# A macaron block on one core: three of four rounds of state powers on GpSimd, slots laid out anew, first constants on ScalarE's queue, the flag read ahead of the last store

## What is computed

```
K = s4d_kernel(log_dt, log_A_real, A_imag, C_real, C_imag, 1024)   # 256 channels x 32 states -> 1024 taps
def conv(x):   y = irfft(rfft(x, 2048) * rfft(K, 2048))[:1024]; return gelu(y) @ W.T + b
def ffn(x):    h = silu(x @ w1.T * s1) * (x @ w2.T * s2)           # 256 -> 1024
               h = gelu(h @ h1.T * t1); h = gelu(h @ h2.T * t2)    # 1024 -> 1024 -> 1024
               return h @ w3.T * s3                                # 1024 -> 256
x = x + 0.5 * ffn(layernorm(x))
x = x + conv(layernorm(x))
x = x + 0.5 * ffn(layernorm(x))
```

## Time and profile before

| | |
|---|---|
| median of 3 runs | 1340.68 us (1340.23 to 1342.07) |
| the profiled execution's own time | 1344.0 us |
| its span, first to last instruction | 1342.2 us |
| mean granted TensorE clock | 0.994 |
| busy: PE, DVE, ACT, POOL | 1318.8, 893.0, 746.7, 382.9 us |

### The profile page before, as it was taken

How to read it: one execution, slowest core, us unless ns; L and a number is a source line. 1 busy time by engine, 2 the same in 40 slices (tenths; PEclk the granted TensorE clock), 3 DMA queues, 4 the chain that set the end, 5 groups by cost and what they waited for, 6 DMA issues and landing times.

```text
span 1342.2 us, 18334 instructions
## 1 busy us (share of the span) xinstructions
PE 1318.8 (98%) x7278; PEld 670.6 (50%) x7278; DVE 893.0 (67%) x1746; ACT 746.7 (56%) x1201; POOL 382.9 (29%) x350
## 2 busy tenths in 40 slices
PE   8999999799999999999999999999999999999997
PEld 3454454455544445455454554545545455454544
DVE  5257869842543877878778787787877873454723
ACT  5474546564447456574665746757467464445422
POOL 5811129500010442614326043260532500001000
PEclk9999999899999999999999999999999999999999
DMA  9210001001010000000100000000000001222300
GB/s 335 97 47 9 9 1 17 1 1 17 0 48 17 0 17 1 9 9 0 17 0 9 16 9 17 17 9 16 9 16 17 9 17 71 69 89 53 136 0 18
DMA packets 44701, 41.88 MB, mean 31 GB/s; under 512 B 32704, under 2 KB 41408, under 8 KB 41920
## 3 DMA queue, kind: packets, MB, share of 16 engines
q1 hardware_dynamic: 44608, 40.64, 10.4%
HBM read 28.57 MB, written 4.19 MB: 24 GB/s over the span
## 4 chain that ended last, share of the span: by engine, by line
PE 92%; DVE 6%; ACT 1%; DMA 1%; issue 1%; SPq 0%; DVEq 0%
PE psf L1339 62%; PE psf L1327 16%; PE psf L1351 8%; PE pss L1402 2%; DVE arena L585 2%; PE pss L1412 2%; PE pss L1392 2%; DVE arena L588 1%; DVE hab L626 1%; PE pss L1382 1%; DMA g<-w 1%; PE pss L1367 0%; DVE arena L597 0%; DVE arena L804 0%; ACT sil L1094 0%
## 5 line engine op out<-in xcount | busy, mean ns | idle before, releaser
L1339 PE MATMUL psf<-hab,wall 128*128 128x512 f16 x4096 | 890.8, 379 | 5.0 <-DVE ht L638 3.1
L1339 PEld LDWEIGHTS psf<-hab,wall 128*128 128x128 f16 x4096 | 399.2, 98 | 486.5 <-issue 7.9
L1111 ACT ACTIVATE psf<-psf,scf 128x512 f32<-128x512 f32 x256 | 168.7, 659 | 428.9 <-PE psf L1339 428.8
L626 DVE SCALAR_TENSOR_TENSOR hab<-psf,hab 128x512 f16<-128x512 f32 x256 | 175.4, 687 | 307.8 <-ACT hab L1104 307.6
L1327 PE MATMUL psf<-h,wall 128*128 128x512 f16 x1024 | 236.1, 384 | 8.3 <-DVE hab L626 6.9
L1327 PEld LDWEIGHTS psf<-h,wall 128*128 128x128 f16 x1024 | 100.5, 99 | 127.0 <-DVE hab L626 8.2
L1104 ACT ACTIVATE hab<-psf 128x512 f16<-128x512 f32 x256 | 152.9, 597 | 8.1
L975 POOL TENSOR_SCALAR rs<-mv 128x4 f32<-128x4 f32 x16 | 3.1, 193 | 506.1 <-DVE mv L669 500.4
L638 DVE SCALAR_TENSOR_TENSOR ht<-psf,scf,sil 128x512 f32<-128x512 f32 x128 | 95.1, 750 | 70.9 <-PE psf L1327 69.3
L1094 ACT ACTIVATE sil<-psf,scf 128x512 f32<-128x512 f32 x128 | 87.3, 686 | 95.3 <-PE psf L1327 93.1
L626 DVE SCALAR_TENSOR_TENSOR hab<-ht,hab 128x512 f16<-128x512 f32 x128 | 116.6, 918 | 3.0
(11 more groups left out here) (130 smaller groups left out, 913.6 us busy)
## 6 DMA issues: line engine op xcount, KB each, us to landing
arena<-wh SPq DMA_DIRECT2D x8, 1024.0 KB, 5.5
g<-wh SPq DMA_DIRECT2D x6, 1024.0 KB, 8.7
out<-xr SPq DMA_DIRECT2D x15, 256.0 KB, 2.2
xr<-x SPq DMA_DIRECT2D x7, 512.0 KB, 5.1
arena<-w SPq DMA_DIRECT2D x3, 1024.0 KB, 5.4
g<-w SPq DMA_DIRECT2D x2, 1024.0 KB, 6.7
xr<-wh SPq DMA_DIRECT2D x2, 1024.0 KB, 10.2
g<-w SPq DMA_DIRECT2D x2, 512.0 KB, 5.9
```

The lines of the kernel that those rows point to most:

```text
L626: e.scalar_tensor_tensor(out=hab[:, buffer(p), m, 1, :], in0=source(p), scalar=2.0 ** E2 if l else 1.0, in1=hab[:, buffer(p), m, 0, :], op ...
L1111: e.activation(bank, bank, ACT.Gelu, scale=scf[:, 2 + l, m:m + 1]).then_inc(s_gelu, 1)
L1339: ins = e.matmul(bank[:, :], WH[:, l, m // 2, k, ms], hab[:, buffer(p), k, part, :], start=(k == 0 and part == 0), stop=(k == KH - 1 and p ...
```

## The change

- `ROUNDS` is `(range(0, 3), range(3, 4))`: POOL makes rounds 0, 1 and 2, DVE round 3 alone. The slots of the spreads and of the groups of matmuls (`SPREAD_AT`, `HALF_AT`) are set anew, so are those of the factors (`FACTORS_HIGH_AT`, `FACTORS_LOW_AT`), the start of `taps` (slot 12 of pass 0) and `TAPS_BESIDE`; ACT's cast of piece 4 moves from slot 6 to slot 8.
- `cs` and the scales `scr` are loaded from ACT's queue, behind its first table load and first activation, not from SP's, where they stood third and seventh. POOL's exponent column is a small tile of its own, `half`. DVE scales `scr` ahead of the first normalisation and not behind the first splits, and the second half of the first weight piece is cast by POOL once the first rows are normalised.
- SP loads the flag into a register between the last store but one and the last, branches, and waits for the stores behind the branch.

```
-CAST_AT = {2: 3, 4: 6, 6: 12, 8: 14, 10: 16}
+CAST_AT = {2: 3, 4: 8, 6: 12, 8: 14, 10: 16}
...
-TAPS_BESIDE = BESIDE[:16] + [0, 0, 0, 0, 1300, 0, 0, 1300, 0, 3000]
-ROUNDS = (range(0, 2), range(2, 4))
+TAPS_BESIDE = BESIDE[:14] + [2000, 0, 0, 0, 0, 0, 1300, 0, 0, 0, 0, 3000]
+ROUNDS = (range(0, 3), range(3, 4))
...
-FACTORS_HIGH_AT, FACTORS_LOW_AT = T(1, 25), T(2, 3)
-SPREAD_AT = ((T(2, 8), T(2, 10), T(2, 20), T(3, 2)), (T(2, 10), T(2, 12), T(2, 23), T(3, 3)))
-HALF_AT = ((T(2, 12), T(2, 14), T(3, 4), T(3, 6)), (T(2, 13), T(2, 15), T(3, 5), T(3, 7)))
+FACTORS_HIGH_AT, FACTORS_LOW_AT = T(1, 20), T(1, 23)
+SPREAD_AT = ((T(2, 2), T(2, 6), T(2, 11), T(2, 13), T(2, 20), T(2, 23)), (T(2, 8), T(2, 9)))
+HALF_AT = ((T(2, 4), T(2, 9), T(2, 14), T(2, 19), T(3, 4), T(3, 6)), (T(2, 11), T(2, 13)))
...
             def taps():
-                yield At(T(0, 14))
+                yield At(T(0, 12))
...
             def powers():
+                yield from factors_low()
                 ch.after()
                 for n, c in enumerate(ROUNDS[1]):
-                    for time in doubled(ch, 1, c):
-                        yield time
-                    if not n:
-                        yield from factors_low()
+                    yield from doubled(ch, 1, c)
...
             sums(0)
-            norm_first()
-            w.wait_ge(s_w0[1], 16)
-            e.tensor_scalar(wall[:, 1024:2048], stage[:, 1024:2048], 1.0, None, ALU.mult).then_inc(s_cast2, 1)
-            for k in range(2):
-                low_first(k)
             w.wait_ge(s_scl, 16)
             for n, e2 in enumerate((-E0, E1 - E0, -E1, -E2)):
                 e.tensor_scalar(scf[:, n, :], scr[:, n, :], 2.0 ** e2, None, ALU.mult).then_inc(s_sc, 1)
             w.wait_ge(s_sc, 4)
+            norm_first()
+            for k in range(2):
+                low_first(k)
...
             strand = Strand(beside())
+            e.memset(half[:, :], -0.5).then_inc(s_halved, 1)
             scales_of(0)
+            w.wait_ge(s_nrm, TPC)
+            w.wait_ge(s_w0[1], 16)
+            e.tensor_copy(wall[:, 1024:2048], stage[:, 1024:2048]).then_inc(s_cast2, 1)
             cast(1)
...
             e.activation(one2[:, :], hab[:, 1, 0, 0, 0:1], ACT.Silu)
+            e.dma_start(cs[:, 0:C_DA], cst[:, 0:C_DA]).then_inc(s_cst, 16)
+            e.dma_start(scr[:, :, :].rearrange("p a k -> p (a k)"), sc).then_inc(s_scl, 16)
             cast_first()
...
             e.dma_start(xr[:, 2:4, :], xv[:, 2:4, :]).then_inc(s_x[0], 16)
-            e.dma_start(cs[:, 0:C_DA], cst[:, 0:C_DA]).then_inc(s_cst, 16)
...
             e.dma_start(small[:, 0:320], ks).then_inc(s_ks, 16)
-            e.dma_start(scr[:, :, :].rearrange("p a k -> p (a k)"), sc).then_inc(s_scl, 16)
...
                     c = i - NC
+                    if i + 1 == PASSES and t0 + n == TPC:
+                        w.wait_ge(s_flag, 1)
+                        e.load(flagged, flag[0:1, 0:1])
                     w.wait_ge(s_xup, 2 * i + g + 1)
...
-            for c in range(NC):
-                w.wait_ge(s_out[c], 16 * len(groups(NC + c)))
...
         def _(e):
-            sp_program(e)
-            unless_exact(e, "sp")
+            with e.register("flag_sp") as r:
+                sp_program(e, r)
+                with e.If_ne(r, 0):
+                    all_out(e)
+                    general(e, "sp")
+            all_out(e)
```

More of the change, by code:

```diff
@@ L331, in build_program @@
         rn = sb("rn", [P, 3, TPC])
+        half = sb("half", [P, TPC])
         bad = sb("bad", [P, 12])
@@ L417, in build_program @@
         s_ln, s_lnc, s_rs, s_rsc = sem("s_ln"), sem("s_lnc"), sem("s_rs"), sem("s_rsc")
+        s_halved = sem("s_halved")
         s_nrm, s_phi, s_plo, s_t0 = sem("s_nrm"), sem("s_phi"), sem("s_plo"), sem("s_t0")
@@ L973, in scales_of @@
                 w.wait_ge(s_ln, 8 * (i + 1))
-                w.wait_ge(s_cst, 16)
                 e.tensor_scalar(r, mv[:, 0, :, 1], EPS, 1.0, ALU.add, ALU.mult).then_inc(s_rs, 1)
@@ L978, in scales_of @@
                 w.wait_ge(s_rs, n + 2 if i else 1)
-                e.tensor_tensor(r, r, cs[:, C_HALF:C_HALF + TPC], ALU.pow).then_inc(s_rs, 1)
+                w.wait_ge(s_halved, 1)
+                e.tensor_tensor(r, r, half[:, :], ALU.pow).then_inc(s_rs, 1)
                 if i:
@@ L987, in conv_scales @@
                 w.wait_ge(s_lnc, 2 * NB * (b + 1))
+                w.wait_ge(s_cst, 16)
                 e.tensor_scalar(r, mv[:, 1:3, :, 1], EPS, 1.0, ALU.add, ALU.mult).then_inc(s_rsc, 1)
@@ L1475, in pe_program, with sp_program @@
             assert all(strand.over for strand in strands)
-        def sp_program(e):
+        def sp_program(e, flagged):
             w = Waits(e)
@@ L1804, in build_program, with all_out @@
         block = ctx.enter_context(nc.Block())
+        def all_out(e):
+            for c in range(NC):
+                e.wait_ge(s_out[c], 16 * len(groups(NC + c)))
         def unless_exact(e, me):
```

## The result

The changed kernel took 1333.68 us (median of 4 executions, 1332.17 to 1335.71), the kernel before 1341.32 beside it: ratio 0.9945, 95% interval 0.9927 to 0.9962. That is 7.6 us faster, by more than the 0.2% that can be told from no change, inside the range given and 4.5 us above the forecast of 1329.2.

A forecast was written before the change was run, and what follows sets the result against it. PE, busy 1318.8 of 1342.2 us, bounds the kernel, leaving its waits, start and end: -9.99 - 1.25 - 0.36 + 0.6 + 2.5 + 0 - 3.0 = -11.5, from the median 1340.68 to 1329.2. Range for 8 in 10: 1325.5 to 1334.

The forecast's parts named there:

- The hole: Up projection behind pass 2: PE's 6.90 us wait for VectorE's low part, plus 3.09 of slowed clock, goes: -9.99 us.
- the two gates: PE's waits for gates on VectorE ahead of passes 1 and 2 go: -1.25 and -0.36 us.
- VectorE's round: Pass 2: VectorE's powers ready at 225.0 us, 0.9 before PE asks for them at 225.9, so no wait.
- the group of slot 9: Pass 2: GpSimd waits for this group of PE's until 222 us, yet is ready by 230, before PE asks at 239.6.
- The wait for ScalarE's copy at slot 13: Pass 2: PE waits 0.6 us for a bank that ScalarE copies out, between 0 and 1.5.
- The new wait behind pass 0: First up projection behind pass 0: earlier taps delay VectorE's low parts of s14 and s15; PE 2.5 us later, 1.5 to 3.5.
- The cast of piece 4: Pass 0: the cast ends at about 40.2 us instead of 28.3, PE wants it at 41.3; no cost, 1 us of slack.
- the lock: Pass 2, slots 16 to 25: GpSimd's third round obstructs VectorE's low parts that read SBUF: +1 us, 1330.2; chance 0.10.
- rival 2: Pass 1: the new 2 us wait makes the clock fall, price 3.1 us, time 1332.3; chance 0.10.
- The start: Up to the first normalisation: loads and VectorE's order changed, taken as 0 us, from +2.0 to -1.0.
- Rival 1: Start: the scales' load holds VectorE until the second weight half has landed: +2.0 us, 1331.2; chance 0.15.
- The end: End of the span: SP's branch of 2.7 us runs beside the last store's 3.0: 3.0 us gained, 1.5 to 3.2.

The follow-up runs named there:

- the powers alone: Kernel before with only the powers and slots changed (rounds, spreads, groups, factors, taps, cast of piece 4): 1336.08 us, ratio 0.9958.
- more of the wait: Changed kernel with the taps' quotas of slots 14 and 15 at 4000 and 2700 instead of 2000 and 0: 1340.65 us, ratio 0.9985.
- the two comparisons: The changed kernel, unaltered, timed twice beside the kernel before: 1333.68 us, ratio 0.9945, then 1332.52 us, ratio 0.9928.

## Why the forecast was right, and where it was off

*The hole, -9.99, and the two gates, -1.25 and -0.36:* right in mechanism, and against the one trace in size: from pass 2's start to pass 4 the two traces differ by 9.8 us. But that trace of the kernel before was of an execution of 1344.0 us, 3.3 over the median from which the forecast subtracts, and "all terms are waits that don't depend on profiling" doesn't hold for the clock in it. Behind the same wait of 6.90 us, 20 matmuls took 7.41 us in it, 5.89 and 6.11 in the two other traces with this stretch unchanged, and 4.5 would be undisturbed: the clock's share is 2.9, 1.4 or 1.6 us, and the hole, with slot 13 in it, is worth 8.3 to 9.8. The timelines of VectorE (the last of its round) and of GpSimd in pass 2:

```profile
226.06 3.19 DVE L603 TENSOR_TENSOR arena<-arena 128x1024 f16<-128x1024 f32 x2
...
227.02 3.14 POOL L599 CAST arena<-arena 128x1024 f16<-128x1024 f32 x2 [3.96 <-PE pss L1373]
```

VectorE's round was ready 43.7 us into pass 2 (229.25 less 185.55), forecast 43.9 (225.0 less 181.07); PE asked at 230.87, 45.3 in. GpSimd waited 3.96 us for the group of slot 9, as forecast, and was ready in time all the same (at 234.8, PE asked at 245.35).

*The wait for ScalarE's copy at slot 13, 0.6:* 0.60. The sum should have taken 0.3, since 0.29 of it stood in the earlier trace rows already.

*The new wait behind pass 0, 2.5:* right in mechanism and size. It is 2.73 in the first trace, 2.26 without the collision (0.36 for s14 and 1.90 for s15, forecast 0.3 and 2.1), and the taps one slot earlier take all of it away. From start to start it costs 2.6 us: the last 16 matmuls begin 61.3 us into pass 0 without the collision and 58.7 before (16 matmuls behind 82.65, less 27.40).

***The cast of piece 4 "costs nothing with 1 us of slack"*** is the step that failed. I looked at PE, who wants the piece at 41.3 us and has it. But the cast is 1.9 us of ScalarE between two tiles, the statistics hang on the second, GpSimd's scales on them and its angles on these, and 1.8 us later GpSimd's product covers the instruction on which the transposes wait. It costs 1.7 us of PE's time, and removing it in two independent ways gives the same 61.3 us. That the result lies inside the range all the same is luck in part: the room above 1329.2 was left for rivals with other causes. The prediction had the lock among them (3), in pass 2 and at 1 us. There PE has no wait behind the groups (its row at 272.99 has none), and the price came in pass 0.

*The clock, rival 2, chance 0.10:* it came true in both traces of the changed kernel (16 matmuls in 6.56 and 5.25 us instead of 3.63: 2.9 and 1.6 us), in that of the powers alone (4.93) and in that with more of the wait (5.32), and not in that with the scales moved. The two traces with only the two later waits (0.36 and 1.90) show 3.63 too. The price was right as an upper bound and the chance far too low: the trace of before showed a fall after one wait of 6.9 us and none after 1.25, and I took the new wait alone, not the three in a row that it became. Whether it was the third wait, which the collision brought, that made the clock fall is argued and not shown.

*The start, 0 between -1.0 and +2.0:* right, in the medians (1.0005 with the start alone). The -1.2 us of the first trace is no gain of the start. Pass 0 started at 26.19 and 24.97 in two traces of the same kernel, at 25.54 with the start unchanged but the cast moved, and at 28.11 at the latest. Most of that scatter is the clock in the first up projection, which the prediction left out: its 64 matmuls took 14.3 us at full clock and 16.89 in the trace that began pass 0 at 28.11. Rival 1 is half true: VectorE stood still for `scr` for 0 to 2.29 us, and no median shows it. The Trainium skill, "DMA: Bandwidth & Descriptors", section "Queues, rings and completion order", has each DMA engine take turns between the queues packet by packet; from that it does not follow that the load comes behind whole half-megabyte pieces, as the prediction read it. It landed 3.3 to 6.6 us after its issue with one small load ahead of it, against 6.6 as the seventh on SP's queue; no run here shows in what order the packets went.

*The end, -3.0:* 2.85 in the trace, 2.7 in the medians.

Put together with the sizes measured, from start to start: -9.8 (hole, slot 13 with it) - 1.4 - 0.5 (gates) + 2.6 (taps) + 1.7 (collision) + 0 (start) - 2.8 (end) + 0.3 (pass 6) = -9.9. With the hole at 8.3 it is -8.4, and the clock behind pass 0 takes 0 to 2.9 us of either, so between -9.9 and -5.5; the two comparisons gave -7.4 and -9.7 by their ratios. The forecast's -11.5 lacked the collision and the clock, and had the hole at its size in a slow execution. The lower bound 1325.5 doesn't follow from its parts either: 1329.2 less 1.0 (start), 1.0 (new wait) and 0.6 (slot 13) is 1326.6.

## What to carry to other kernels

A work item that is moved has two effects: when its result is there, and what it pushes back on its own engine. Follow the second through every wait to the engines that never see the result; here a cast on ScalarE shifted GpSimd by 1.8 us onto an instruction of VectorE's, and PE paid 1.7 us for it. Before, the two had met by 0.1 us at no cost, so there was no slack to push them together; that could be read from the trace of before. Before work is put into an engine's idle time, look at what shares its memory ports in that time: 0.63 us became 2.38. Where three short waits come close together, allow for the clock: it fell in four of five such traces here. And a term read from one trace holds for that execution; where the clock is in it, look at a second trace before it is taken from a median.

## What was not expected of the hardware

A VectorE instruction with both inputs in SBUF can be held for nearly the whole of a GpSimd instruction (0.69 became 2.40 to 2.43 beside one of 2.08), a one-operand step on float32 too (0.63, 2.38), while the low parts that read PSUM stayed at 0.68 beside the same work; those that read `ht`, with both inputs in SBUF, took up to 2.11 in the changed kernel (at 186.42). ScalarE's two DMAs, which its program has behind the first activation, were issued at 1.19 and 1.67 us, during the table load (0.72 to 2.00). And the same idle times, 3.8 us in 8, were followed by a granted clock of 1.2 GHz for 6.8 us, for 3.4 us or not at all, in executions of nearly the same kernel.
